# The mix slots of a recurrent-attention kernel: one ScalarE pass and a VectorE read of the transposed bank

## The chip, the cores and the metric

The kernel runs on one core of a Trainium2 chip. The metric is the time of the whole kernel on the device, in microseconds (us). Before the change its median over three runs is 988.88 us (988.46 to 989.01).

## The reference

What is computed, cut to its core (x is 8 batches of 1024 tokens with 512 channels):

```
xn  = layernorm(x)
xs  = xn shifted by one token (zero in front)
xm  = xn * time_mix + xs * (1 - time_mix)
k   = exp(min(xm @ Wk.T, 60));  v = xm @ Wv.T;  r = xm @ Wr.T
wkv, sum_k = decayed sums over earlier tokens of k*v and of k   (per head)
out = x + (sigmoid(r) * wkv / sum_k) @ Wo.T
        + ternary_linear(quantised(layernorm_affine(xn)))       (needs the largest |value| of all tokens)
```

The quantised linear layer needs one maximum over all of its input, so a batch can be finished only after a look at all batches.

## The kernel before

Channels are put on the 128 partitions in four chunks (ch 0 to 3), and 512 tokens make a tile, two tiles for a batch. TensorE transposes a chunk of a normalised tile into PSUM, the result is evacuated, and the projections multiply it. Every projection uses a high and a low part of each operand, three matmuls for one product.

The work goes over the eight batches in order. Batches 0 to 3 are phase A, where the feed-forward slots are only looked at for their maximum, and batches 4 to 7 are phase B, where the feed-forward output is computed as well (also for batches 0 to 3, whose attention result was parked in memory). Each batch is a row of 24 groups g. In group g, TensorE does one slot (four 128x128 transposes, `slot`, L342) and then one projection of 12 matmuls (`project`, L403 to L405; k, v and r in turn, m = g mod 3). In group 12 the projection comes first. After groups 4, 8, 16 and 20 of phase B, a feed-forward product of 32 matmuls follows (`ffn_out`, L436 and L438); after group 12 and at the end of the batch comes an attention output of 48 matmuls (`attn_out`, L418 to L420).

The 24 slots of a batch are, four of each: ffn_own0 (0 to 3), ffn_other0 (4 to 7), mix_own1 (8 to 11), ffn_own1 (12 to 15), ffn_other1 (16 to 19), mix_next0 (20 to 23; they belong to the next batch, and the last batch has none). With four slots of the prologue there are 64 mix slots.

All slots but the prologue's share one PSUM bank, `TB` ("transposed"). TensorE may write slot n+1 into it once slot n has been read. In the kernel before, the reader is ScalarE (`evacuate`): a mix slot takes two passes over the bank, L485 (times time_mix, into `U`, "evacuated") and L486 (times one minus time_mix, into `WS`, "shifted_part"), and the second one raises `act_u`. TensorE waits for `act_u` before each slot. VectorE (`mix_or_clip`) adds the two with a shift of one token: L722 keeps the last column for the next tile (tile 0) or L724 adds the kept column (tile 1), L725 adds columns 1 to 511 and raises `dve_x`. ScalarE then rounds the high part (`high_part`, L525), and VectorE subtracts it (`low_part`, L749), which raises `dve_lo`. `U` and `WS` have two places each, and slot n+2 may be evacuated after `low_part` of slot n.

Each engine works through its own list in order. VectorE's list is written out by hand in `batch`, from L854 on. In a group with m = 1 it has `rwkv` (L818) and then `recurrence`: the product k*v (L792), two scans (L802), and a combination of both sums (L809). In a group with m = 2 it starts with `rwkv_lo` (L822), and `mix_or_clip` of the group's slot comes next. `STATS_AT` puts the statistics of a tile (L677, L682) into groups 4 and 16. ScalarE's list has `evacuate`, `high_part` of the slot before, `exp_k` (L574), `ln_sums` (L585), `quotient` (L590), `rwkv_hi` (L604) and `exp_r` (L578, L581) in the order of the groups.

Of the kernel before, what the change touches and what calls it, by code (L numbers as in the profile page):

```python
# [24 lines left out]
ALU = mybir.AluOpType  # L25
ACT = mybir.ActivationFunctionType
AX = mybir.AxisListType

P = 128
TILE = 512  # L30
# [14 lines left out]
SLOTS = [(kind, ch) for kind in SLOT_KINDS for ch in range(4)]  # L45
# [10 lines left out]
def mixed_decay_kernel(nc, x, time_decay, time_first, time_mix, Wk, Wv, Wr, Wo, Wf, ln_gamma, ln_beta, out):  # L56
    B, T, C = x.shape
    H = time_decay.shape[0]
    CH = C // P
# [14 lines left out]
    with ExitStack() as ctx:  # L74
        def sb(name, shape, dt=F32):
            return ctx.enter_context(nc.sbuf_tensor(name, shape, dt))

        def sem(name):
            return ctx.enter_context(nc.semaphore(name))
# [12 lines left out]
        U = sb("evacuated", [P, 2, TILE])  # L92
        WS = sb("shifted_part", [P, 2, TILE])
# [11 lines left out]
        tmx = sb("time_mix", [P, CH])  # L105
# [8 lines left out]
        last_x = sb("last_token", [P, CH])  # L114
# [18 lines left out]
        TB = ctx.enter_context(nc.psum_tensor("transposed", [P, TILE], F32))  # L133
# [42 lines left out]
        dve_x = sem("dve_mixed_or_clipped")  # L176
# [25 lines left out]
        def slots_before(b, ph, n):  # L202

            return n if ph == "P" else CH + len(SLOTS) * b + n

        def splits_before(b, ph, n):


            if ph == "P":
                return n  # L210
            if ph == "A":
                return CH + 2 * CH * b + sum(kind.startswith("mix") for kind, _ in SLOTS[:n])
            return CH + 2 * CH * HALF + len(SLOTS) * (b - HALF) + n
# [4 lines left out]
        def slot_of(ph, n):  # L218
            return ("mix_next0", n) if ph == "P" else SLOTS[n]

        def first_slot(kind):
            return SLOTS.index((kind, 0))

        def normed_count(b, kind):


            return 4 * b + [k for k in SLOT_KINDS if "other" not in k].index(kind) + 1
# [22 lines left out]
        first_banks = [TB[:, :]] + [KVR[:, i, :] for i in range(3)]  # L250
# [81 lines left out]
        def _(pe):  # L332
# [4 lines left out]
            def transpose_slot(b, ph, n, src):  # L337

                _, ch = slot_of(ph, n)
                bank = first_banks[n] if ph == "P" else TB[:, :]  # L340
                for q in range(Q):
                    last = nc.tensor.transpose(bank[:, q * P:(q + 1) * P], src[:, q, ch * P:(ch + 1) * P],  # L342
                                               ident[:, :])
                last.then_inc(pe_t, 1)
# [9 lines left out]
            for n in PROLOGUE:  # L354
# [7 lines left out]
                for ch in range(CH):  # L362
                    if unit >= len(weight_banks):
                        pe.wait_ge(dve_w, unit - len(weight_banks) + 1)
                    bank = weight_banks[unit % len(weight_banks)]
# [4 lines left out]
                    unit += 1  # L370
            pe.wait_ge(dve_w, CH)
            pe.wait_ge(act_u, CH)

            def slot(b, ph, n):
                kind, _ = slot_of(ph, n)
                pe.wait_ge(act_u, slots_before(b, ph, n))
                if n % CH == 0:

                    if "other" in kind:
                        for normed in (pool_za, act_za):  # L380
                            pe.wait_ge(normed, 2 * b + int(kind[-1]) + 1)
                    else:
                        for normed in (pool_xn, act_xn):
                            pe.wait_ge(normed, CREDIT + normed_count(b, kind))
                transpose_slot(b, ph, n, ZA if "other" in kind else XN)
# [59 lines left out]
            def batch(b, ph, is_last=False):  # L445
                for g in range(GROUPS):
                    n = slot_ahead(g, is_last)
                    if g == ATTN0_AFTER:
                        project(b, ph, g)
                        slot(b, ph, n)  # L450
                    else:
                        if n is not None:
                            slot(b, ph, n)
                        project(b, ph, g)
                    if ph == "B" and g in FFN_AFTER:
                        ffn_out(b, FFN_AFTER[g])
                    if g == ATTN0_AFTER:
                        attn_out(b, ph, 0)
                attn_out(b, ph, 1)
# [10 lines left out]
        def _(act):  # L470
# [5 lines left out]
            def evacuate(b, ph, n):  # L476

                kind, ch = slot_of(ph, n)
                bank = first_banks[n] if ph == "P" else TB[:, :]
                m = slots_before(b, ph, n)  # L480
                act.wait_ge(pe_t, m + 1)
                act.wait_ge(dve_lo, m + 1)
                r = n % 2
                if kind.startswith("mix"):
                    nc.scalar.activation(U[:, r, :], bank, ACT.Copy, scale=tmx[:, ch:ch + 1])  # L485
                    nc.scalar.activation(WS[:, r, :], bank, ACT.Copy,  # L486
                                         scale=tmx1[:, ch:ch + 1]).then_inc(act_u, 1)
                elif ph == "A":

                    nc.scalar.activation(U[:, r, :], bank, ACT.Identity, bias=bet[:, ch:ch + 1],  # L490
                                         scale=gam[:, ch:ch + 1]).then_inc(act_u, 1)
                else:

                    nc.scalar.activation(U[:, r, :], bank, ACT.Identity, bias=betq[:, ch:ch + 1],  # L494
                                         scale=gamq[:, ch:ch + 1]).then_inc(act_u, 1)
# [54 lines left out]
            for n in PROLOGUE:  # L550
                if n == "slots":
                    act.wait_ge(dve_c, 4)
                    for pair in range(0, CH, 2):
                        for m in (pair, pair + 1):
                            evacuate(0, "P", m)
                        for m in (pair, pair + 1):
                            high_part(0, "P", m)
                    nc.scalar.activation(decay[:, :], decay[:, :], ACT.Exp, scale=-1.0).then_inc(act_c, 1)
                    continue
                for ch in range(CH):  # L560
                    act.wait_ge(pe_w, unit + 1)
                    nc.scalar.activation(WH[n][:, ch, :], weight_banks[unit % len(weight_banks)],
                                         ACT.Copy).then_inc(act_w, 1)
                    unit += 1
                if n == "k":
                    act.wait_ge(dve_c, 3)
                    nc.scalar.activation(first[:, :], first[:, :], ACT.Exp)
                    nc.scalar.activation(decay[:, :], decay[:, :], ACT.Exp).then_inc(act_c, 1)
                    act.wait_ge(act_c, 1)
# [88 lines left out]
        def _(dve):  # L658
            V = nc.vector
# [53 lines left out]
            def mix_or_clip(b, ph, n):  # L713

                kind, ch = slot_of(ph, n)
                m = slots_before(b, ph, n)
                r = n % 2
                dve.wait_ge(act_u, m + 1)
                if kind.startswith("mix"):

                    if kind.endswith("0"):
                        V.tensor_copy(last_x[:, ch:ch + 1], WS[:, r, TILE - 1:TILE])  # L722
                    else:
                        V.tensor_tensor(U[:, r, 0:1], U[:, r, 0:1], last_x[:, ch:ch + 1], ALU.add)  # L724
                    V.tensor_tensor(U[:, r, 1:TILE], U[:, r, 1:TILE], WS[:, r, 0:TILE - 1],  # L725
                                    ALU.add).then_inc(dve_x, 1)
                elif ph == "A":

                    if n == 0:
                        dve.wait_ge(dve_mx, b + 1)  # L730
                    col = n if n < first_slot("mix_own1") else n - CH
                    V.tensor_reduce(am[:, col:col + 1], U[:, r, :], AX.X, ALU.max,
                                    apply_absolute_value=True).then_inc(dve_lo, 1)
                else:
                    V.tensor_scalar(U[:, r, :], U[:, r, :], QB - FFN_EPS, -QB + FFN_EPS, ALU.min,
                                    ALU.max).then_inc(dve_x, 1)
# [117 lines left out]
            def batch(b, ph, is_last=False):  # L854
                last = None
                for g in range(GROUPS):
# [5 lines left out]
                    if part1_first:  # L862
                        mix_or_clip(b, ph, n)
# [10 lines left out]
                    if n is not None and not part1_first:  # L874
                        mix_or_clip(b, ph, n)
# [168 lines left out]
```

## Time and profile before

| | before |
|---|---|
| median of three runs | 988.88 us |
| lowest and highest | 988.46, 989.01 us |
| span of the profiled execution | 987.2 us |
| median less that span | 1.7 us |
| TensorE busy | 936.3 us, 95% |
| VectorE busy | 806.9 us, 82% |
| ScalarE busy | 549.3 us, 56% |
| GpSimd busy | 278.9 us, 28% |

The time is that of an unprofiled run, the span goes from the first to the last instruction of one profiled execution. A batch of phase A repeats every 102.1 us and one of phase B every 132.4 us, so the start of one batch tells where the same event of the next one lies.

### The profile page before, as it was taken

To read this page: it belongs to the slowest core of one execution; us is meant where nothing else is said; L and a number is where in the kernel's file an instruction comes from. 1 tells how busy PE (TensorE), PEld (TensorE's weight loads), DVE (VectorE), ACT (ScalarE), POOL (GpSimd) and SP (SyncE) were. 2 spreads that over 40 slices of the span, in tenths; PEclk is the share of its full clock that TensorE was granted. 3 is DMA by queue.
4 is the path that set the end of the run, shared out by engine and by line. 5 is a ranking of instruction groups with operands and counts; after the bars stand their busy time and mean duration, and the time that the engine had idled before them with its cause. 6 is when DMAs were issued, how large, how long until landed. Compare 5 with 4: busy or idle time off the path is not lost.

```text
span 987.2 us, 14552 instructions
## 1 busy us (share of the span) xinstructions
PE 936.3 (95%) x4418; PEld 757.4 (77%) x4418; DVE 806.9 (82%) x1418; ACT 549.3 (56%) x881; POOL 278.9 (28%) x428
## 2 busy tenths in 40 slices
PE   5589999999999999997999999999999999999998
PEld 4478778777877787775787877887878778788786
DVE  5788988889888989895788787797888787878875
ACT  5365756666665757474554454646555546556432
POOL 4332424152415232432303314024023050230300
PEclk9889999999999999999999999999999999999999
DMA  8010302030302121213104113131131221320302
GB/s 317 24 43 25 104 31 97 0 127 0 111 17 86 41 85 42 85 42 128 37 34 144 43 44 129 42 128 63 64 129 42 85 85 42 106 72 36 129 1 85
DMA packets 36560, 72.81 MB, mean 74 GB/s; under 512 B 1180, under 2 KB 1192, under 8 KB 36520
## 3 DMA queue, kind: packets, MB, share of 16 engines
q1 hardware_dynamic: 36520, 72.36, 20.9%
q8 instruction: 14, 0.23, 0.1%
q14 instruction: 26, 0.21, 0.1%
HBM read 47.19 MB, written 25.17 MB: 73 GB/s over the span
## 4 chain that ended last, share of the span: by engine, by line
PE 41%; DVE 28%; issue 14%; ACT 10%; DMA 4%; POOL 2%; DVEq 0%; ACTq 0%; SPq 0%; POOLq 0%
PE kvr L403 7%; PE kvr L405 7%; PE kvr L404 7%; DVE scans L802 7%; PE out_banks L436 5%; PE out_banks L438 5%; PE transposed L342 4%; DVE bn_stats L677 3%; PE out_banks L418 3%; PE out_banks L420 2%; PE out_banks L419 2%; DVE rwkv_lo L822 2%; DVE k_and_kv L792 2%; DVE k_and_kv L818 2%; DVE evacuated L725 2%
## 5 line engine op out<-in xcount | busy, mean ns | idle before, releaser
L968 POOL TENSOR_SCALAR normed<-x,own_stats 128x512 f32<-128x512 f32 x68 | 88.7, 1312 | 239.2 <-PE transposed L342 231.9
L948 POOL TENSOR_SCALAR stat_work<-mean_var 128x4 f32<-128x4 f32 x32 | 10.9, 339 | 344.8 <-DVE mean_var L682 319.8
L403 PE MATMUL kvr<-xm_hi,wv_hi 128*128 128x512 f32 x256 | 107.4, 419 | 0.0
L403 PE MATMUL kvr<-xm_hi,wk_hi 128*128 128x512 f32 x256 | 106.5, 416 | 0.0
L403 PE MATMUL kvr<-xm_hi,wr_hi 128*128 128x512 f32 x256 | 105.8, 413 | 0.0
L418 PE MATMUL out_banks<-wo_hi,rwkv_hi 128*128 128x512 f32 x256 | 103.0, 402 | 2.4 <-DVE rwkv_lo L822 2.4
L405 PE MATMUL kvr<-xm_hi,wv_lo 128*128 128x512 f32 x256 | 101.7, 397 | 0.0
L420 PE MATMUL out_banks<-wo_hi,rwkv_lo 128*128 128x512 f32 x256 | 101.2, 395 | 0.0
L419 PE MATMUL out_banks<-wo_lo,rwkv_hi 128*128 128x512 f32 x256 | 101.2, 395 | 0.0
L436 PE MATMUL out_banks<-w_ternary,ffn_hi 128*128 128x512 f32 x256 | 100.4, 392 | 0.7 <-DVE ffn_lo L749 0.5
L404 PE MATMUL kvr<-xm_lo,wv_hi 128*128 128x512 f32 x256 | 100.9, 394 | 0.0
L405 PE MATMUL kvr<-xm_hi,wk_lo 128*128 128x512 f32 x256 | 100.7, 393 | 0.0
L405 PE MATMUL kvr<-xm_hi,wr_lo 128*128 128x512 f32 x256 | 100.6, 393 | 0.0
L404 PE MATMUL kvr<-xm_lo,wk_hi 128*128 128x512 f32 x256 | 100.1, 391 | 0.0
L438 PE MATMUL out_banks<-w_ternary,ffn_lo 128*128 128x512 f32 x256 | 99.7, 390 | 0.0
L404 PE MATMUL kvr<-xm_lo,wr_hi 128*128 128x512 f32 x256 | 99.7, 389 | 0.0
L494 ACT ACTIVATE evacuated<-transposed,beta_scaled,gamma_scaled 128x512 f32<-128x512 f32 x64 | 49.3, 770 | 72.8 <-PE transposed L342 68.5
L342 PE MATMUL transposed<-ident,normed 128*128 128x128 f32 x500 | 76.0, 275 | 10.9 <-ACT evacuated L490 4.7
L809 DVE SCALAR_TENSOR_TENSOR k_and_kv<-k_and_kv,first,scans 128x1024 f32<-128x1024 f32 x64 | 84.7, 1323 | 1.1
L342 PEld LDWEIGHTS transposed<-ident,normed 128*128 128x128 f32 x500 | 60.6, 140 | 32.1 <-POOL normed L968 6.7
L490 ACT ACTIVATE evacuated<-transposed,beta_in,gamma_in 128x512 f32<-128x512 f32 x64 | 49.4, 771 | 63.2 <-PE transposed L342 57.3
L802 DVE TENSOR_TENSOR_SCAN scans<-decay,state,k_and_kv 128x512 f32<-128x512 f32 x64 | 80.0, 1292 | 0.0
(126 smaller groups left out, 2151.3 us busy)
## 6 DMA issues: line engine op xcount, KB each, us to landing
x<-in_L_attn_x SPq DMA_DIRECT2D x16, 1024.0 KB, 5.3
other<-in_L_attn_x SPq DMA_DIRECT2D x16, 1024.0 KB, 5.3
attn_scratch<-x SPq DMA_DIRECT2D x8, 1024.0 KB, 4.3
parked<-attn_scratch SPq DMA_DIRECT2D x8, 1024.0 KB, 6.7
out<-parked SPq DMA_DIRECT2D x8, 1024.0 KB, 4.3
out<-x SPq DMA_DIRECT2D x7, 1024.0 KB, 4.4
parked<-in_L_attn_Wk SPq DMA_DIRECT2D x1, 1024.0 KB, 7.9
other<-in_L_attn_Wv SPq DMA_DIRECT2D x1, 1024.0 KB, 10.1
```

The lines of the kernel that those rows point to most:

```text
L342: last = nc.tensor.transpose(bank[:, q * P:(q + 1) * P], src[:, q, ch * P:(ch + 1) * P], ident[:, :])
L403: nc.tensor.matmul(KVR[:, m, :], hi, XH[t][:, ch, :], start=(ch == 0), stop=False)
L404: nc.tensor.matmul(KVR[:, m, :], hi, XL[t][:, ch, :], start=False, stop=False)
L405: last = nc.tensor.matmul(KVR[:, m, :], lo, XH[t][:, ch, :], start=False, stop=(ch == CH - 1))
L418: nc.tensor.matmul(OUT[:, q, :], hi, WH["o"][:, j, :], start=(j == 0), stop=False)
L419: nc.tensor.matmul(OUT[:, q, :], hi, WL["o"][:, j, :], start=False, stop=False)
L420: last = nc.tensor.matmul(OUT[:, q, :], lo, WH["o"][:, j, :], start=False, stop=(j == CH - 1))
L436: nc.tensor.matmul(OUT[:, q, :], AH[:, ch, q * P:(q + 1) * P], WQ[:, ch, :], start=(ch == 0), stop=False)
L438: last = nc.tensor.matmul(OUT[:, q, :], AL[:, ch, q * P:(q + 1) * P], WQ[:, ch, :], start=False, stop=(ch == CH - 1))
L802: last = V.tensor_tensor_scan(S[:, i, 1:TILE + 1], dec, kv[:, i, :], 0.0 if t == 0 else state[:, j, i:i + 1], ALU.mult, ALU.add)
L809: V.scalar_tensor_tensor(kv, kv, first[:, j:j + 1], S[:, :, 0:TILE], ALU.mult, ALU.add).then_inc(dve_sum, 1)
L968: last = G.tensor_scalar(dst[:, q, :], src[:, q, :], stats[:, 2 * ffn, q:q + 1], stats[:, 2 * ffn + 1, q:q + 1], ALU.mult, ALU.add)
```

## The change

A mix slot has one ScalarE pass (into `WS`) in place of two. VectorE's instruction that added `U` and `WS` becomes one that reads the bank, multiplies it by time_mix and adds the shifted `WS` (`scalar_tensor_tensor`). The first column is treated in the same way: tile 1 has a `scalar_tensor_tensor` in place of the one-column addition, and tile 0 gets a one-column `tensor_scalar` that it didn't have. Since VectorE now reads the bank too, TensorE waits for `dve_x` as well as `act_u` before a slot that follows a mix slot (slots 0, 9 to 12 and 21 to 23), and once before the first batch.

```diff
             pe.wait_ge(dve_w, CH)
             pe.wait_ge(act_u, CH)
+            pe.wait_ge(dve_x, CH)
 
             def slot(b, ph, n):
                 kind, _ = slot_of(ph, n)
                 pe.wait_ge(act_u, slots_before(b, ph, n))
+                if n == 0 or SLOTS[n - 1][0].startswith("mix"):
+
+                    pe.wait_ge(dve_x, splits_before(b, ph, n))
...
                 if kind.startswith("mix"):
-                    nc.scalar.activation(U[:, r, :], bank, ACT.Copy, scale=tmx[:, ch:ch + 1])
                     nc.scalar.activation(WS[:, r, :], bank, ACT.Copy,
                                          scale=tmx1[:, ch:ch + 1]).then_inc(act_u, 1)
...
                 if kind.startswith("mix"):
 
+                    bank = first_banks[n] if ph == "P" else TB[:, :]
                     if kind.endswith("0"):
                         V.tensor_copy(last_x[:, ch:ch + 1], WS[:, r, TILE - 1:TILE])
+                        V.tensor_scalar(U[:, r, 0:1], bank[:, 0:1], tmx[:, ch:ch + 1], None, ALU.mult)
                     else:
-                        V.tensor_tensor(U[:, r, 0:1], U[:, r, 0:1], last_x[:, ch:ch + 1], ALU.add)
-                    V.tensor_tensor(U[:, r, 1:TILE], U[:, r, 1:TILE], WS[:, r, 0:TILE - 1],
-                                    ALU.add).then_inc(dve_x, 1)
+                        V.scalar_tensor_tensor(U[:, r, 0:1], bank[:, 0:1], tmx[:, ch:ch + 1],
+                                               last_x[:, ch:ch + 1], ALU.mult, ALU.add)
+                    V.scalar_tensor_tensor(U[:, r, 1:TILE], bank[:, 1:TILE], tmx[:, ch:ch + 1],
+                                           WS[:, r, 0:TILE - 1], ALU.mult, ALU.add).then_inc(dve_x, 1)
```

## Rows read from the trace of the kernel before

**Rows 1.** The page's busy us of each engine (share of the span), instructions.

```profile
PE 936.3 (95%) x4418; PEld 757.4 (77%) x4418; DVE 806.9 (82%) x1418; ACT 549.3 (56%) x881; POOL 278.9 (28%) x428
```

**Rows 2.** Windows, phases A and B: length, busy PE, PEld, DVE, ACT, POOL; clock, DMA.

```profile
202.00:304.00 102.00, 100.32 (x481) 80.70 (x480) 90.06 (x158) 63.37 (x100) 35.37 (x52) 1.00 0.17 61
...
622.00:755.00 133.00, 130.41 (x613) 105.46 (x612) 107.48 (x189) 72.34 (x118) 32.74 (x52) 1.00 0.23 79
```

**Rows 3.** Timeline (start, length, engine, line [idle before <-releaser]), TensorE, slots 8 to 11.

```profile
270.87 0.30 PE L342 MATMUL transposed<-ident,normed 128*128 128x128 f32 x1 [0.47 <-ACT evacuated L490]
...
274.09 0.27 PE L342 MATMUL transposed<-ident,normed 128*128 128x128 f32 x1
...
277.30 0.27 PE L342 MATMUL transposed<-ident,normed 128*128 128x128 f32 x1
...
280.79 0.33 PE L342 MATMUL transposed<-ident,normed 128*128 128x128 f32 x1
```

**Rows 4.** Timeline, VectorE, batch 2: from the product of group 7 to slot 8.

```profile
272.13 0.68 DVE L792 TENSOR_TENSOR k_and_kv<-k_and_kv,kvr 128x512 f32<-128x512 f32 x1
...
276.39 0.68 DVE L822 TENSOR_TENSOR rwkv_lo<-k_and_kv,rwkv_hi 128x512 fp32r<-128x512 f32 x1
...
277.06 0.68 DVE L725 TENSOR_TENSOR evacuated<-evacuated,shifted_part 128x511 f32<-128x511 f32 x1
```

**Rows 5.** Timeline, ScalarE, batch 2: the second pass of slot 10.

```profile
280.05 0.68 ACT L486 ACTIVATE shifted_part<-transposed,one_minus_mix 128x512 f32<-128x512 f32 x1
```

**Rows 6.** Timeline, batch 2: VectorE at slot 20, then TensorE's slot 21.

```profile
328.25 0.68 DVE L725 TENSOR_TENSOR evacuated<-evacuated,shifted_part 128x511 f32<-128x511 f32 x1
...
325.22 0.27 PE L342 MATMUL transposed<-ident,normed 128*128 128x128 f32 x1
```

**Rows 7.** Timeline, batch 0: VectorE at slot 8, then TensorE's slot 9.

```profile
72.51 0.68 DVE L725 TENSOR_TENSOR evacuated<-evacuated,shifted_part 128x511 f32<-128x511 f32 x1
...
70.42 0.27 PE L342 MATMUL transposed<-ident,normed 128*128 128x128 f32 x1
```

**Rows 8.** Lines by form, VectorE (busy us, mean ns of one | idle before).

```profile
L841 DVE TENSOR_TENSOR x<-x,out_banks 128x512 f32<-128x512 f32 x64 | 39.6, 677 | 2.2 <-PE out_banks L420 2.2
...
L843 DVE SCALAR_TENSOR_TENSOR x<-out_banks,scalars,x 128x512 f32<-128x512 f32 x32 | 23.1, 743 | 0.0
...
L722 DVE COPY last_token<-shifted_part 128x1 f32<-128x1 f32 x32 | 4.8, 150 | 15.6 <-ACT shifted_part L486 15.4
```

**Rows 9.** Timeline, phase B, batch 5: VectorE at slots 8 and 10, TensorE's slots 9 and 11.

```profile
631.70 0.68 DVE L725 TENSOR_TENSOR evacuated<-evacuated,shifted_part 128x511 f32<-128x511 f32 x1
...
640.85 0.69 DVE L725 TENSOR_TENSOR evacuated<-evacuated,shifted_part 128x511 f32<-128x511 f32 x1
...
634.99 0.38 PE L342 MATMUL transposed<-ident,normed 128*128 128x128 f32 x2
...
641.39 0.38 PE L342 MATMUL transposed<-ident,normed 128*128 128x128 f32 x2
```

**Rows 10.** Timeline, the waits of attn_out: phase A, then phase B.

```profile
343.88 0.50 PE L418 MATMUL out_banks<-wo_hi,rwkv_hi 128*128 128x512 f32 x1 [0.16 <-DVE rwkv_lo L822]
...
719.84 0.50 PE L418 MATMUL out_banks<-wo_hi,rwkv_hi 128*128 128x512 f32 x1 [0.57 <-DVE rwkv_lo L822]
```

**Rows 11.** Timeline, TensorE and GpSimd in the prologue and batch 0.

```profile
26.95 0.45 PE L342 MATMUL transposed<-ident,normed 128*128 128x128 f32 x1 [3.94 <-POOL normed L968]
...
31.51 0.27 PE L342 MATMUL transposed<-ident,normed 128*128 128x128 f32 x1
...
39.75 0.33 PE L342 MATMUL transposed<-ident,normed 128*128 128x128 f32 x1 [1.67 <-ACT evacuated L490]
...
32.51 0.40 POOL L981 PARTITION_ALL_REDUCE scalars<-scalars  x1 [5.71 <-issue]
```

**Rows 12.** Windows after the starts at 26.95 and 39.75.

```profile
27.00:28.00 1.00, 1.00 (x5) 1.00 (x6) 0.93 (x2) 0.64 (x3) 0.00 (x0) 0.50 0.00 0
...
40.00:41.00 1.00, 1.00 (x8) 0.87 (x7) 1.00 (x3) 0.00 (x0) 0.00 (x0) 1.00 0.00 0
```

## The prediction

> **What bounds the kernel.** I read the page's busy times first, then the windows of a batch of each phase, the waits of TensorE, and then the timeline around the mix slots. TensorE is busy 936.3 of 987.2 us [rows 1] and 98% of a window in both phases at full clock (100.3 of 102.0 and 130.4 of 133.0 us) [rows 2]: TensorE's list sets the time. ScalarE has 62% in phase A, VectorE 88% (63.4 and 90.1 of 102) [rows 2]. So 0.7 us less on ScalarE is worth nothing by itself. What counts is when TensorE may write the transposed bank again, and that is now decided on VectorE as well, the fuller of the two, whose list is in order.
>
> **The order around a mix slot.** In phase A slots 8, 9 and 10 start at 270.87, 274.09 and 277.30 [rows 3], 3.2 us apart, which is four transposes and 12 matmuls: slot 9 follows the projection of group 8 without idle time. ScalarE has read the bank by then; the latest it gets is at slot 10, where its second pass ends at 280.73 [rows 5] and slot 11 starts at 280.79 [rows 3]. VectorE comes to slot 8 much later. Its list has the recurrence of group 7 first: the product at 272.13, two scans, the combination, then L822 at 276.39, and only then L725, 277.06 to 277.74 [rows 4]. This chain starts from the projection of group 7, which ends as slot 8 starts (270.87); the 6.9 us from there to 277.74 can't be beaten by the 3.2 us that TensorE has to spend on slot 8 and its projection. Before the change that delay cost nothing, because the bank had been read by ScalarE and U had a second place.
>
> **Terms of the sum.**
>
> 1. Two ScalarE passes become one: 64 x 0.68 us [rows 5], up to 44 us of an engine that has room. Gain by itself: 0. It brings the VectorE instruction forward only where that one waited for ScalarE.
>
> 2. The VectorE instruction. The trace has no scalar_tensor_tensor of this form. A scalar_tensor_tensor of 512 columns with a PSUM operand takes 743 ns, an addition with a PSUM operand 677 ns [rows 8], and L725 takes 0.68 us [rows 4]. The nearest row is the first, so I add 0.06 us, with 0 as the other end; nothing in the rows makes it faster than the addition. The extra one-column instruction of slots 20 to 23 is like the copy L722, 150 ns [rows 8]; it overlaps its neighbour, so that I take 0.07 us, between 0 and 0.15. Release from VectorE to TensorE: 0.06 us, as from ScalarE (280.73 to 280.79 [rows 3, 5]; bound: 0 to 0.1).
> The Trainium skill (Perfetto Trace Analysis, section Optimizing Scalar/DVE Operations) gives VectorE about 65 ns more per instruction on PSUM than on SBUF. The additions here don't show it (677 ns with a PSUM operand against 0.68 us), the scalar_tensor_tensor does; by the rule the new instruction would cost 0.065 us more, and the sum would move by less than 0.1 us.
>
> 3. **The new wait, slots 9 and 21 of phase A** (8 events). TensorE may start slot 9 at 277.74 + 0.06 + 0.06 = 277.86 in place of 274.09: 3.77 us later. In batch 0 VectorE is nearer: L725 ends at 73.19, slot 9 started at 70.42 [rows 7], so 2.89. Batches 1 and 3 have 3.81 and 3.77 by the same reading. Sum of slot 9: 14.2 us. For slot 21, L725 of slot 20 ends at 328.93 and the slot started at 325.22 [rows 6]: 3.71 + 0.06 + 0.07 + 0.06 = 3.90; the four batches agree within 0.02, so 15.6 us. Together **+29.8 us**. Behind the waiting transposes lie the projection and all later work of TensorE, which is the bound, so the whole of it reaches the end. Neither VectorE nor ScalarE is what it then waits for: both only catch up.
>
> 4. **Slots 10 to 12, 22, 23 and 0.** After the stall ScalarE and VectorE have nothing left over. Group 9 starts with the mix instruction and slot 10 has 3.2 us. For slot 11 phase B is the pattern, since slot 9 comes there after a rest too: VectorE's L725 of slot 10 begins at 640.85 and ends at 641.54, and slot 11 starts at 641.39 [rows 9]. Without the first ScalarE pass it begins 0.55 us sooner (bounded by what VectorE does before), and ends 0.2 us before slot 11. No stall in either phase. Slots 12 and 0 come behind two projections or 48 matmuls.
>
> 5. **Given back.** In phase A slot 11 starts 3.49 us after slot 10 and not 3.21 [rows 3], since ScalarE's second pass is late. That 0.28 to 0.30 occurs seven times (slots 11 and 23) and goes away: -2.1 us. The last quarter of attn_out waits 0.16 us for L822 in phase A [rows 10], 0.3 with the break in the pipeline, four times. VectorE's chain behind slot 22 starts 0.9 us sooner against TensorE, so this goes too: -1.3. The passage from phase A to B hangs on the same chain: -0.3.
>
> 6. **Phase B.** Slot 9 starts at 634.99, and L725 of slot 8 ended at 632.38 [rows 9]: the feed-forward product in between covers the wait, 2.6 us of room, and slot 21 has the same. If that cover were gone, phase A's price would apply. The slower instruction delays ffn_lo by 0.13 us three times (+0.4), the shorter chain gives back about 0.3 of the 0.57 us waits in rows 10. Net +0.1.
>
> 7. **Prologue.** The four slots finish about 1.5 us sooner, but slot 0 waits for GpSimd until 26.95, and the all-reduce at 32.51, on which everything to slot 4 hangs, starts after 5.71 us in which GpSimd waits for nothing shown [rows 11]. Value 0, bounds -1.5 and 0.
>
> 8. **Clock.** TensorE came back from 3.94 us of idle time at 1.2 GHz (granted 0.50), and from 1.67 us at 2.4 GHz (1.00) [rows 11, 12]. From the slow start, slot 0 to slot 1 took 4.56 us (26.95 to 31.51) against 3.2: one fall costs 1.36 us. The new idle stretches are 0.16 us shorter than the delays (a matmul's end lies that much behind the next start): 3.6 to 3.75 us seven times and 2.7 once, just under the one that fell. Bounds 0 and 8 x 1.36 = 10.9; I take one fall, +1.4.
>
> Sum: 29.8 - 2.1 - 1.3 - 0.3 + 0.1 + 1.4 = 27.6. Against the profiled execution: 987.2 + 27.6 = 1014.8 of span, and the median lies 1.7 above the span: 1016.5 us, or 2.8% slower. Own range 1012 to 1020 (0 to 3 falls, 0.06 us of the instruction eight times, half of term 5).
>
> **Rivals.**
>
> - *The clock falls at most stalls.* 3.65 us is near 3.94. Then up to 9.5 us more than with one fall: 1021 to 1026. For it: the stretches are alike in length and distance, so they may fall or hold together; against it: all are shorter than the only short one that fell. The Trainium skill (TensorE: Matmul & The Clock Gate, section HAM oscillation) tells of just such a kernel, in which every wait between bursts brings the clock down. By that rule the time is 1026; rows 12 bear out that it can happen.
> - *The stall is shorter.* VectorE's product starts at 272.13, 1.26 us after the projection was ready [rows 3, 4]. Were that lateness a backlog which the stalls clear, each would be 1.2 us less: 1007. Against it: each batch makes the lateness anew, by the statistics in groups 4 and 16, ahead of the stalls.
> - *Faster.* The wait is hidden after all because VectorE reaches the slot within 3.2 us, and only terms 5 and 7 stay: 988.9 - 3.7 - 1.5 = 983.7. It decides at a delay below about 0.5 us for each stall, where +29.8 has to shrink to the 3.7 given back. It needs VectorE to take the mix before the recurrence, which its list doesn't allow.
> - *The change does nothing to the order* (the wait is met, since the counts of `dve_x` come a slot early). Then about 985 to 989. The counts in `splits_before` speak against it.
>
> **Chances.** Forecast 0.70 (1012 to 1020); clock at most stalls 0.12; shorter stalls 0.11; faster 0.04; nothing 0.03, split between faster and the same. A difference under 0.2% (2 us) can't be told from none. The range that leaves out under 2 in 10 reaches from 1009 to 1026. Faster 0.05, same 0.02, slower 0.93.
>
> **What the new profile would show.** Eight idle stretches of TensorE ahead of L342, 3.6 to 3.8 us (one 2.7), released by the new VectorE line, all in phase A; phase A's batch longer by 6.8 us (108.9), phase B's by less than 0.3; the new instruction near 743 ns; the waits of L342 for L486 gone; ScalarE busy 36 to 44 us less (passes overlap a little); L981 still at 32.5. I am wrong if the new wait shows in phase B, if slots 10, 11 or 22 stall too (each 0.1 us of an unseen delay there costs 0.8), or if the granted clock is 0.50 after each stall.

## The result and the profile after

The changed kernel takes 1028.09 us (1027.05 to 1029.56, four runs) against 988.81 us: the ratio is 1.040, with an interval of 1.039 to 1.042. That is 39.3 us more. The forecast was 1016.5 us and its range ended at 1026: direction right, size wrong. The profiled execution took 1029.56 us, with a span of 1027.7 us, 40.5 us more than the span before.

The page of the changed kernel, to be read beside [rows 1]: its busy times, the granted clock in 40 slices, and the attention output's wait.

```profile
PE 950.6 (92%) x4418; PEld 772.7 (75%) x4418; DVE 814.8 (79%) x1450; ACT 515.3 (50%) x817; POOL 271.1 (26%) x428
...
PEclk9789989998999899998999999999999999999999
...
L422 PE MATMUL out_banks<-wo_hi,rwkv_hi 128*128 128x512 f32 x256 | 102.2, 399 | 0.6 <-DVE rwkv_lo L828 0.6
```

ScalarE is 34.0 us less busy (36 to 44 were forecast), which by itself moves nothing. TensorE has the same 4418 matmuls and is 14.3 us *more* busy: the same work took longer, and in the clock's line four slices of the first half have an 8 where they had a 9, and one has a 7 where it had an 8. The attention output waits 0.6 us for VectorE in the whole run: the waits that [rows 10] show for phase A are gone. The list of waits of the changed kernel (us in total, times, longest) has a row that didn't exist:

```profile
PE transposed L342 <- DVE evacuated L731: 33.1, 9, 4.1
```

Nine waits: one of 4.1 us in the prologue (there GpSimd was waited for before, 3.94 us [rows 11]) and eight in phase A. Batch 2 on TensorE's timeline, which answers to [rows 3], starts of slots 8, 9, 10 and 11:

```profile
290.85 0.63 PE L342 MATMUL transposed<-ident,normed 128*128 128x128 f32 x4 [0.46 <-ACT evacuated L493]
...
297.89 1.08 PE L342 MATMUL transposed<-ident,normed 128*128 128x128 f32 x4 [3.66 <-DVE evacuated L731]
302.75 0.60 PE L342 MATMUL transposed<-ident,normed 128*128 128x128 f32 x4
305.94 0.60 PE L342 MATMUL transposed<-ident,normed 128*128 128x128 f32 x4
```

and VectorE's, which answers to [rows 4]:

```profile
292.11 0.68 DVE L798 TENSOR_TENSOR k_and_kv<-k_and_kv,kvr 128x512 f32<-128x512 f32 x1
...
296.36 0.69 DVE L828 TENSOR_TENSOR rwkv_lo<-k_and_kv,rwkv_hi 128x512 fp32r<-128x512 f32 x1
...
297.09 0.74 DVE L731 SCALAR_TENSOR_TENSOR evacuated<-transposed,time_mix,shifted_part 128x511 f32<-128x511 f32 x1
```

Slot 9 starts 7.04 us after slot 8 and not 3.22, because L731 ends at 297.83. This is the wait that was foreseen. Then comes what wasn't: slot 10 starts 4.86 us after slot 9, and not 3.21, though nothing is waited for. The four transposes of slot 9 take 1.08 us, those of slots 10 and 11 0.60. After slot 21 it is longer still; slots 21 and 22 of the same batch:

```profile
354.06 1.12 PE L342 MATMUL transposed<-ident,normed 128*128 128x128 f32 x4 [3.79 <-DVE evacuated L731]
359.79 0.60 PE L342 MATMUL transposed<-ident,normed 128*128 128x128 f32 x4
```

The windows of TensorE (length, busy us, granted clock, DMA) say why:

```profile
298.00:299.00 1.00, 1.00 (x5) 0.50 0.00 0
...
302.00:303.00 1.00, 1.00 (x7) 1.00 0.00 0
...
353.00:354.00 1.00, 0.00 (x0) 0.50 0.00 0
354.00:357.00 3.00, 2.94 (x9) 0.50 0.00 0
357.00:359.00 2.00, 2.00 (x6) 0.50 0.00 0
359.00:360.00 1.00, 1.00 (x6) 0.80 0.00 0
```

TensorE runs at 1.2 GHz (0.50) from the end of the stall to 301.4, and at the second stall until past 359.

**The whole difference by steps.** I set the distance from each slot's start to the next against the same distance before. The four steps from slot 8 to 9 are 2.95, 3.82, 3.82 and 3.82 us longer, those from 20 to 21 3.97, 3.94, 3.95 and 3.95: 30.2 us of waiting. The four from 9 to 10 are 1.63 to 1.65 us longer and those from 21 to 22 2.79, 2.66, 2.51 and 2.53: 17.0 us of slow clock. Together 47.2, and 6.7 us are given back elsewhere; that is the 40.5 us of the span.

### The profile page after: what moved, and what is told of

Its sections match the earlier page's. It is cut to its first block, busy times and chain, and to the rows that moved or that the text cites. A ratio compares the mean times of both kernels' runs of the same rounds, so it can differ in the third digit from the quotient of the medians.

```text
span 1027.7 us, 14541 instructions
## 1 busy us (share of the span) xinstructions
PE 950.6 (92%) x4418; PEld 772.7 (75%) x4418; DVE 814.8 (79%) x1450; ACT 515.3 (50%) x817; POOL 271.1 (26%) x428
## 4 chain that ended last, share of the span: by engine, by line
PE 49%; DVE 26%; issue 14%; ACT 7%; POOL 2%; DMA 1%; DVEq 0%; ACTq 0%; SPq 0%; POOLq 0%
PE kvr L407 8%; PE kvr L409 8%; PE kvr L408 8%; DVE scans L808 7%; PE transposed L342 4%; PE out_banks L422 4%; PE out_banks L424 4%; PE out_banks L423 4%; PE out_banks L440 4%; PE out_banks L442 4%; DVE bn_stats L680 2%; DVE k_and_kv L798 2%; DVE rwkv_lo L828 2%; ACT evacuated L497 2%; DVE evacuated L731 1%
## 5 line engine op out<-in xcount | busy, mean ns | idle before, releaser
L974 POOL TENSOR_SCALAR normed<-x,own_stats 128x512 f32<-128x512 f32 x68 | 85.0, 1258 | 286.3 <-PE transposed L342 279.4
L342 PE MATMUL transposed<-ident,normed 128*128 128x128 f32 x500 | 78.9, 282 | 38.9 <-DVE evacuated L731 33.1
L407 PE MATMUL kvr<-xm_hi,wk_hi 128*128 128x512 f32 x256 | 112.6, 440 | 0.0
L342 PEld LDWEIGHTS transposed<-ident,normed 128*128 128x128 f32 x500 | 62.8, 144 | 60.0 <-DVE evacuated L731 32.3
L409 PE MATMUL kvr<-xm_hi,wk_lo 128*128 128x512 f32 x256 | 106.1, 414 | 0.0
L408 PE MATMUL kvr<-xm_lo,wk_hi 128*128 128x512 f32 x256 | 106.0, 414 | 0.0
L489 ACT ACTIVATE shifted_part<-transposed,one_minus_mix 128x512 f32<-128x512 f32 x61 | 41.9, 686 | 90.1 <-PE transposed L342 87.6
```

The costliest lines, as they stand in the source:

```text
L407: nc.tensor.matmul(KVR[:, m, :], hi, XH[t][:, ch, :], start=(ch == 0), stop=False)
L408: nc.tensor.matmul(KVR[:, m, :], hi, XL[t][:, ch, :], start=False, stop=False)
L409: last = nc.tensor.matmul(KVR[:, m, :], lo, XH[t][:, ch, :], start=False, stop=(ch == CH - 1))
L974: last = G.tensor_scalar(dst[:, q, :], src[:, q, :], stats[:, 2 * ffn, q:q + 1], stats[:, 2 * ffn + 1, q:q + 1], ALU.mult, ALU.add)
```

## The experiments

**The wait alone.** The kernel before, with TensorE's new wait and nothing else:

```diff
+            pe.wait_ge(dve_x, CH)
...
+                if n == 0 or SLOTS[n - 1][0].startswith("mix"):
+                    pe.wait_ge(dve_x, splits_before(b, ph, n))
```

> The kernel before with TensorE's new wait alone; ScalarE keeps its two passes and VectorE its addition, which still takes its operand from SBUF. Theory (the loss is where the wait is released): slots 9 and 21 of phase A start some 3.7 to 3.8 us late as in the changed kernel, the granted clock falls to 1.2 GHz in some or all of these stalls, and nothing is given back: 1012 us with no fall, 1029 with the falls of the changed kernel. Rival (the new instruction, which reads PSUM, or VectorE's extra work is what costs): at most 990 us.

Measured: 1028.2 us (1028.06 to 1028.86), ratio 1.040 (1.038 to 1.042). The wait alone makes the loss, with VectorE's instruction, its operands and ScalarE's passes as they were before. That the two times are equal is in part luck. By the same count of steps in the profiled execution, the eight delays add to 29.1 us (the mix instruction is a little shorter), the clock fell at seven of the eight stalls and cost 13.8 us, and 3.6 us came back: less was lost to the clock and less was given back, and the two nearly cancel.

**No read of the bank.**

```diff
-            pe.wait_ge(dve_x, CH)
...
-                if n == 0 or SLOTS[n - 1][0].startswith("mix"):
-
-                    pe.wait_ge(dve_x, splits_before(b, ph, n))
...
-                    bank = first_banks[n] if ph == "P" else TB[:, :]
+                    bank = WS[:, r, :]
```

> The changed kernel without TensorE's new waits: the scalar_tensor_tensor takes its first operand from the shifted SBUF copy and not from the bank, so the mixed values are wrong (it computes with the copy scaled by one minus time_mix). The number of passes and instructions is that of the changed kernel. Theory: no stall is left and what the saved passes give back remains, 982 to 985 us. Rival (the instruction costs): above 989 us, with VectorE the engine that TensorE waits for in other places.

Measured: 985.42 us, ratio 0.997 (0.996 to 0.998). VectorE takes the shifted copy in the bank's place here, so the unshifted values are left out of the mix. All that the change could give, were the bank free in time, is 3.4 us.

**Work for TensorE inside the stall.**

```diff
                         project(b, ph, g)
+                    if ph == "A" and g in (8, 20):
+                        pe.wait_ge(dve_w, 4 * CH)
+                        pe.wait_ge(dve_out, bank_use(b, ph, "attn0" if g == 8 else "attn1") + 1)
+                        for _ in range(12 if g == 8 else 12):
+                            nc.tensor.matmul(OUT[:, 0, :], WH["k"][:, 0, 0:P], WH["k"][:, 1, :],
+                                             start=True, stop=True)
```

> The changed kernel with 12 matmuls of 512 columns that nobody reads, put on TensorE right behind the projections of groups 8 and 20 of phase A, ahead of the transposes that wait: 2.7 us of work inside each stall of 2.8 to 3.8 us. Theory (stall and clock are two losses): the delay of slots 9 and 21 stays, the granted clock stays at 2.4 GHz, the steps from slot 9 to 10 and 21 to 22 fall back to 3.2 us, and the time drops by the 17 us that these steps lost, to 1011 us. Rival (the slow steps are not the clock's, or the fillers lengthen the stalls): 1028 us or more.

Measured: 1012.31 us (1011.6 to 1013.23), 15.8 us below the changed kernel with 96 matmuls *more*. Its slots 8, 9 and 10 of batch 2 on TensorE's timeline, and a window of a batch:

```profile
282.20 0.63 PE L342 MATMUL transposed<-ident,normed 128*128 128x128 f32 x4 [0.46 <-ACT evacuated L499]
289.23 0.66 PE L342 MATMUL transposed<-ident,normed 128*128 128x128 f32 x4 [0.93 <-DVE evacuated L737]
292.48 0.60 PE L342 MATMUL transposed<-ident,normed 128*128 128x128 f32 x4
```

```profile
172.00:285.00 113.00, 109.23 (x524) 88.62 (x523) 96.40 (x169) 62.51 (x97) 35.50 (x59) 1.00 0.17 65
```

The delay of slot 9 is the same (7.03 us after slot 8), the clock is 1.00, and slot 10 follows after 3.25 us. So there are two losses, and they can be taken apart: the delay of 30 us and the clock's 16 to 17.

**Less filling.** The same with 5 matmuls (`range(5 if g == 8 else 5)`).

> The changed kernel with 5 in place of 12 unread matmuls inside each of the eight stalls: 1.1 us of work, so that 1.7 us (batch 0, slot 9) and 2.5 to 2.7 us of idle time are left. Theory (the delay is fixed by VectorE's list, the clock by what TensorE does meanwhile): the delays stay at 3.8 us, and the time is 1012 us if the clock holds, and up to 1028 us for each stall in which it still falls, 1.6 to 2.7 us a fall. Rival (the fillers themselves cost): above 1012 us with the clock at 2.4 GHz throughout.

Measured: 1016.22 us, with a wide spread (1014.46 to 1019.08). In the profiled execution three of eight stalls lost the clock. Two stalls of nearly the same length, starts of slots 21 and 22 in batches 0 and 1 on TensorE's timeline:

```profile
126.38 0.66 PE L342 MATMUL transposed<-ident,normed 128*128 128x128 f32 x4 [2.66 <-DVE evacuated L737]
131.22 0.60 PE L342 MATMUL transposed<-ident,normed 128*128 128x128 f32 x4
```

```profile
238.00 0.66 PE L342 MATMUL transposed<-ident,normed 128*128 128x128 f32 x4 [2.64 <-DVE evacuated L737]
241.26 0.60 PE L342 MATMUL transposed<-ident,normed 128*128 128x128 f32 x4
```

After 2.66 us of idle time the step was 4.84 us, after 2.64 us it was 3.26; slot 9 of batch 1 in the same run lost the clock after only 2.56 us. Length alone doesn't decide. The run with the wait alone shows the same at its longest stalls, slots 21 and 22 of batches 1 and 2, with the windows behind them:

```profile
241.31 0.66 PE L342 MATMUL transposed<-ident,normed 128*128 128x128 f32 x4 [3.59 <-DVE evacuated L728]
244.55 0.60 PE L342 MATMUL transposed<-ident,normed 128*128 128x128 f32 x4
...
352.77 1.12 PE L342 MATMUL transposed<-ident,normed 128*128 128x128 f32 x4 [3.59 <-DVE evacuated L728]
357.38 0.60 PE L342 MATMUL transposed<-ident,normed 128*128 128x128 f32 x4
```

```profile
242.00:246.00 4.00, 4.00 (x21) 1.00 0.00 0
353.00:356.00 3.00, 3.00 (x11) 0.55 0.00 0
```

Both stalls were 3.59 us long, and one kept 2.4 GHz.

**The mix instruction earlier in VectorE's list.**

```diff
-            def recurrence(b, c):
+            def recurrence(b, c, inside=None):
...
                 V.tensor_tensor(kv[:, 1, :], kv[:, 0, :], KVR[:, 1, :], ALU.mult).then_inc(dve_kv, 1)
+                if inside is not None:
+                    mix_or_clip(b, "A", inside)
...
-                    if part1_first:
+                    if part1_first and not (ph == "A" and n in (8, 20)):
                         mix_or_clip(b, ph, n)
...
-                            recurrence(b, c)
+                            recurrence(b, c, g + 1 if ph == "A" and g in (7, 19) else None)
```

> The changed kernel with VectorE's list altered at two places of phase A: the mix instruction of slots 8 and 20 stands right behind the product of groups 7 and 19, ahead of the scans, and no longer behind rwkv_lo. Theory (the place in VectorE's list makes the stall): the bank is free some 0.5 us before slot 9 and 21 need it, no stall and no fall of the clock, what was given back stays: 981 to 986 us, faster than the kernel before. Rival (any VectorE release of the bank is too late, or the recurrence that is pushed back by 0.75 us becomes the wait): between 990 and 1010 us.

Measured: 993.26 us (992.38 to 993.45), ratio 1.004 (1.003 to 1.006). The stall before slots 9 and 21 is gone and 35 us come back, but the time is the rival's. TensorE's slots 8 to 11 of batch 1, and VectorE's mix of slot 9:

```profile
169.69 0.63 PE L342 MATMUL transposed<-ident,normed 128*128 128x128 f32 x4 [0.47 <-ACT evacuated L493]
172.91 0.60 PE L342 MATMUL transposed<-ident,normed 128*128 128x128 f32 x4
177.53 0.66 PE L342 MATMUL transposed<-ident,normed 128*128 128x128 f32 x4 [1.25 <-DVE evacuated L731]
180.79 0.60 PE L342 MATMUL transposed<-ident,normed 128*128 128x128 f32 x4
```

```profile
176.73 0.74 DVE L731 SCALAR_TENSOR_TENSOR evacuated<-transposed,time_mix,shifted_part 128x511 f32<-128x511 f32 x1
```

Slot 10 is 1.4 us late now. The recurrence and rwkv_lo lie ahead of the mix of slot 9, which holds the bank for slot 10. The wait moved by one slot. To settle that, slots 9 and 21 got their two ScalarE passes back and no wait for VectorE behind them (`two_passes` below, with `n in (9, 21)`):

> The run in which the mix instruction of slots 8 and 20 of phase A stands right behind the product, but slots 9 and 21 of phase A keep ScalarE's two passes and no wait for VectorE follows them. That run had removed the stall before slots 9 and 21 and showed a new one of 1.4 to 1.6 us before slots 10 and 22. Theory (the wait has moved by one slot, because the recurrence now lies ahead of the mix of slot 9): with that release back on ScalarE it is gone, 983 to 987 us. Rival (the recurrence that is pushed back by 0.8 us delays the projections by another way): 990 us or more.

Measured: 985.77 us, ratio 0.9974 (0.9965 to 0.9983): the moved wait was the whole rest.

**In between.** The same edit as the earlier mix, but behind the scans:

```diff
                 last.then_inc(dve_scan, 1)
+                if inside is not None:
+                    mix_or_clip(b, "A", inside)
```

> The changed kernel with the mix instruction of slots 8 and 20 of phase A behind the two scans of groups 7 and 19 and ahead of the combination. Theory (the delay is what VectorE's list holds before the mix instruction): by the trace of the changed kernel the bank is free some 5.7 us after slot 8 began, 2.4 to 2.5 us after TensorE would have used it; slot 10 has no wait, since the mix of slot 9 now comes late by less than the delay. Eight delays of 2.4 us on 984 us: 1003 to 1005 us as long as the clock holds. If an idle stretch of 2.3 us also costs the clock (the 2.8 us stretch of batch 0 in the changed kernel did), up to 13 us more.

Measured: 997.8 us (997.78 to 1000.1). Slots 9 and 21 are 1.8 to 2.0 us late (0.9 in batch 0), less than my 2.4, which had overrated the stretch from the scans' start to the mix; the seven delays and the one add to 14.4 us. The order of the times follows the delay: none, 985; 1.9 us, 998; 3.9 us, 1012 with the clock held. Slots 21 and 22 of batch 0, and windows after this stall and after the same one of batch 1:

```profile
122.39 0.93 PE L342 MATMUL transposed<-ident,normed 128*128 128x128 f32 x4 [1.83 <-DVE evacuated L731]
127.23 0.60 PE L342 MATMUL transposed<-ident,normed 128*128 128x128 f32 x4
```

```profile
123.00:126.00 3.00, 3.00 (x9) 0.50 0.01 3
...
229.00:232.00 3.00, 3.00 (x16) 1.00 0.00 0
```

Even 1.83 us of idle time lost the clock once in eight.

**The change only where it is free.** Slots 8, 9, 20 and 21 of phase A as before the change:

```diff
+        def two_passes(ph, n):
+            return ph == "A" and n in (8, 9, 20, 21)
...
-                if n == 0 or SLOTS[n - 1][0].startswith("mix"):
+                if n == 0 or (SLOTS[n - 1][0].startswith("mix") and not two_passes(ph, n - 1)):
...
+                    if two_passes(ph, n):
+                        nc.scalar.activation(U[:, r, :], bank, ACT.Copy, scale=tmx[:, ch:ch + 1])
```

> The changed kernel, but slots 8, 9, 20 and 21 of phase A keep ScalarE's two passes and VectorE's addition, and TensorE doesn't wait for VectorE before slots 9, 10, 21 and 22 of phase A. Theory (the change costs only where VectorE's list holds a recurrence before the release): no stall is left anywhere, the 0.3 us pauses before slots 11 and 23 are gone, the prologue's 1 us is kept: 984 to 986 us, faster than both kernels by 0.3% or more over the one before. Rival (the release on VectorE costs at slots 11, 23 and in phase B too): 989 us or more.

Measured: 986.58 us (nine executions from 985.23 to 987.26; a tenth took 2163.01 us, has no trace, and stays unexplained), ratio 0.9975 (0.9965 to 0.9985). Faster than both kernels, by less than I expected: slots 11 and 23 wait a little longer than before the change. Slot 11 of batch 1:

```profile
177.87 0.66 PE L345 MATMUL transposed<-ident,normed 128*128 128x128 f32 x4 [0.53 <-DVE evacuated L743]
```

Two last runs put slots 10 and 22 back as well, one on this kernel and one on the one with the earlier mix.

> Like the run with ScalarE's two passes kept at slots 8, 9, 20 and 21 of phase A, but slots 10 and 22 keep them as well, so that in phase A only slots 11 and 23 are in the new form. That run had left a wait of 0.5 to 0.57 us for VectorE before slots 11 and 23 (before the change: 0.12 to 0.18 us for ScalarE). Theory (each release on VectorE costs what its list is late at that place): these seven waits fall back to 0.12 to 0.18 us, 2.5 us less: 984 to 985 us. Rival (what is left of the gain comes from ScalarE's saved passes): at or above the 986.6 us of that run.

> Like the run in which the mix of slots 8 and 20 of phase A stands behind the product and slots 9 and 21 keep two passes, but slots 10 and 22 keep them as well. Theory: the waits of 0.27 to 0.44 us before slots 11 and 23 fall to 0.18 us or less, 984 to 985.5 us. Rival (they stay, since ScalarE's second pass is then what comes late): 985.5 to 986.5 us.

Measured: 987.26 us (ratio 0.9991, 0.9982 to 1.0000), a miss, and 985.59 us (0.9974, 0.9965 to 0.9984), just above the expected 985.5, which in number is the rival's range, and not to be told from the 985.77 us. The waits before slots 11 and 23 did fall in both, by 0.3 to 0.45 us each, but the wait of attn_out at the end of a batch came back, 0.35 to 0.38 us, where [rows 10] had 0.16, and the step to the next batch's slot 0 became 0.6 us longer; in the last kernel, batch 1:

```profile
239.90 0.50 PE L425 MATMUL out_banks<-wo_hi,rwkv_hi 128*128 128x512 f32 x1 [0.35 <-DVE rwkv_lo L842]
```

So each batch of phase A gains 0.1 to 0.2 us, and not 0.8: what is won at one place is lost again at the next where VectorE is late. The first of the two has a further loss in its trace that has nothing to do with these slots as far as is seen: in batch 4 TensorE was still at 1.2 GHz (0.50) from 472 to 474 us, where the run with two passes at slots 8, 9, 20 and 21 had 0.91, and slot 5 came 1.2 us later after slot 4. Whether its other executions had this isn't known, so its miss is explained only in part.

## Why the prediction was wrong

- **What bounds the kernel; term 1.** Right. ScalarE's saved passes are worth 3.4 us in all, measured without the wait, and only through what comes sooner behind them.
- **Term 2, the instruction.** Right. Lines by form of the changed kernel:

```profile
L731 DVE SCALAR_TENSOR_TENSOR evacuated<-transposed,time_mix,shifted_part 128x511 f32<-128x511 f32 x61 | 45.3, 742 | 0.0
...
L729 DVE SCALAR_TENSOR_TENSOR evacuated<-transposed,time_mix,last_token 128x1 f32<-128x1 f32 x32 | 6.9, 215 | 22.2 <-ACT shifted_part L489 22.2
L727 DVE TENSOR_SCALAR evacuated<-transposed,time_mix 128x1 f32<-128x1 f32 x29 | 6.1, 211 | 0.0
```

  742 ns against 743 forecast. But one reading behind the number was wrong: the prediction said that the scalar_tensor_tensor shows the extra time of a PSUM operand. In the run without the read of the bank both operands lie in SBUF, and it isn't faster:

```profile
L727 DVE SCALAR_TENSOR_TENSOR evacuated<-shifted_part,time_mix 128x511 f32<-128x511 f32 x64 | 48.7, 760 | 0.0
```

  So the 0.06 us go with the operation and not with PSUM, as far as these rows show. The one-column forms take 211 to 215 ns and not the copy's 150, about 0.05 us more in the chain.
- **Term 3, the new wait.** Right in place, number and size: eight events, 30.2 us against 29.8.
- **Terms 4, 6 and 7.** Right for the slots that term 4 names, and in phase B: none of them waits for VectorE's mix, but for the slot 0 that follows the prologue. Slot 20 of batches 1 to 3 waits 0.83 us for ScalarE now, where it had under 0.3; slot 16 comes 0.6 us sooner, and the two about cancel. The ffn_lo delay is there (0.36 us at its longest). Slot 4 of batch 0 starts 1.1 us sooner (50.96 against 52.08), where I took 0 with -1.5 as the bound; the all-reduce that I held fixed at 32.51 starts at 30.61.
- **Term 5, given back.** 3.7 us forecast; with the 1.3 us up to slot 8 of batch 0, the batch ends (-0.5 each) and phase B, 6.7 came back. Not all of it is due to the saved passes: 3.6 came back with the wait alone, which saves none.
- **Term 8, the clock. This step failed.** I wrote "I take one fall, +1.4". All eight stalls lost the clock, which the prediction had named as a sign of being wrong, and a fall cost 1.64 us after slot 9 and 2.5 to 2.8 us after slot 21, not 1.36: 17.0 us, above even my upper bound of 10.9. Two errors lie in it. First, I took the shortest idle stretch that was seen to fall, 3.94 us, for a threshold, on one event, with one event of 1.67 us that held. The runs show falls after 1.83, 2.56, 2.66 and 2.80 us and a stall of 3.59 us that held. Second, I priced a fall from the one stretch in which half speed ended soon after the restart, and made that price the bound. There it lasted 2.8 us from the restart; in batch 2 of the changed kernel it lasted 3.5 us behind slot 9 and 5.3 us behind slot 21. The rival in which the clock falls at most stalls was right in kind (chance 0.12), and its 1021 to 1026 fell short by the price. With 17.0 in place of 1.4, 6.7 in place of 3.6 and 30.2 in place of 29.8, the sum is 1016.5 + 15.6 - 3.1 + 0.4 = 1029.4, against 1029.6 in the profiled execution that these terms come from (1028.1 in the median).

The Trainium skill (TensorE: Matmul & The Clock Gate, section HAM oscillation) describes a kernel in which every wait between bursts costs the clock again; the changed kernel does just that, eight times of eight. I had given that reading one chance in eight. The other runs don't bear it out in full: the wait alone lost the clock at seven stalls of eight, 5 fillers at three.

The other rivals fell: the delay was not shorter (3.82 to 3.97 us, 2.95 in batch 0 at slot 9), and nothing was hidden. That VectorE's order makes the stall is shown by the runs with the mix moved; that the wait is the cause, by the run with the wait alone.

**Open:** why the changed kernel lost the clock at every stall and the run with the wait alone at all but one, while the runs with 5 fillers and with the shorter stall kept it at most. With the slow stretches the changed kernel's batch is 112.7 to 112.9 us long and each stall of a kind follows the last at that distance, so what holds at one may well hold at the next; no run here tests that.

## What to carry to other kernels

When a buffer's release moves to another engine, look at what stands ahead of the releasing instruction in that engine's list, and not at how busy the engine is: here 5 us of recurrence and rwkv_lo stood in front of a 0.74 us instruction. If the buffer has a single place, count from the event that starts that list's work to the release, and set it against what the bound engine can do meanwhile; a change may still pay at the slots where this is positive, as the mixed version shows. And when TensorE is the bound, a stall of about 2 us or more (the shortest that lost the clock here was 1.83 us) has to be priced twice, as a delay and as matmuls at 1.2 GHz behind it, and the second price may be half of the first (17.0 against 30.2 us here); work that keeps the engine going in the stall takes that part away.

## What the runs showed of the hardware

The batch 0 stall of the changed kernel is the clearest: TensorE was idle for 2.80 us until 72.10, and the clock fell after it had resumed. Windows around it (length, busy us of each engine, granted clock, DMA):

```profile
71.00:72.00 1.00, 0.00 (x0) 0.00 (x0) 1.00 (x3) 0.00 (x0) 0.00 (x0) 1.00 0.00 0
72.00:73.00 1.00, 0.90 (x6) 0.81 (x7) 0.04 (x1) 0.21 (x1) 0.00 (x0) 0.84 0.00 0
73.00:74.00 1.00, 1.00 (x4) 0.81 (x3) 0.49 (x2) 0.99 (x2) 0.00 (x0) 0.50 0.00 0
```

The granted clock is still 1.00 in the last whole microsecond of the stall, and 0.84 in the next, of which only the first 0.1 us was idle. So a fall need not come within the idle time. Nor is it settled by the length of it: 1.83 us lost the clock in one run, 3.59 us kept it in another. Matmuls that nobody reads, put into the stalls, made the kernel faster by 15.8 us. And the scalar_tensor_tensor of 511 columns took 742 ns with a PSUM operand and 760 ns with SBUF operands alone.
